# Sums and norms as stages of their own, a down product in two fp32r parts, and the next head's rows placed beside the linear attention

## The reference

```
x = x + xattn(layernorm(x), ctx, ctx)      # softmax attention, 16 heads of 16, 4096 keys
x = x + linear_attn(layernorm(x))          # causal; features exp(clip(norm(q) @ omega ...)), cumulative sums
x = x + ffn(layernorm(x))
# ffn: gate = x @ wg.T; up = x @ wu.T; h = silu(gate) * up; h @ wd.T
#      wg, wu: 768 x 256 and wd: 256 x 768, integers in -127..127, scaled by 1/127
```

## Time and profile before

| what | value |
|---|---|
| median of 3 timed runs | 877.69 us (876.39 to 878.99) |
| the profiled execution | 875.48 us |
| its span, first to last instruction | 873.8 us (873.76) |
| around the span | 1.7 us |
| PE busy | 829.1 us, 95% |
| PE weight loads busy | 569.8 us, 65% |
| ACT busy | 541.5 us, 62% |
| DVE busy | 417.2 us, 48% |
| POOL busy | 47.1 us, 5% |
| mean granted clock of TensorE | 0.990 |

### The profile page before, as it was taken

How to read it: one execution, slowest core, us unless ns; L and a number is a source line. 1 busy time by engine, 2 the same in 40 slices (tenths; PEclk the granted TensorE clock), 3 DMA queues, 4 the chain that set the end, 5 groups by cost and what they waited for, 6 DMA issues and landing times.

```text
span 873.8 us, 20543 instructions
## 1 busy us (share of the span) xinstructions
PE 829.1 (95%) x8817; PEld 569.8 (65%) x8817; DVE 417.2 (48%) x746; ACT 541.5 (62%) x598; POOL 47.1 (5%) x76
## 2 busy tenths in 40 slices
PE   6899999999999998999999998999999999989876
PEld 5666666666666666676666665667666666657656
DVE  7433236444644445534654446354474444402654
ACT  2478887776577665667567764575657666672141
POOL 1034000000000000000000000000000000000010
PEclk9899999999999999999999999999999999999999
DMA  7486654646344333346343441443614333202000
GB/s 248 172 258 237 241 183 166 209 158 193 122 146 146 142 125 133 122 133 191 136 146 145 146 142 53 158 158 129 195 65 170 122 122 119 100 2 50 0 2 15
DMA packets 58768, 120.08 MB, mean 137 GB/s; under 512 B 21552, under 2 KB 29744, under 8 KB 55152
## 3 DMA queue, kind: packets, MB, share of 16 engines
q1 hardware_dynamic: 56880, 114.31, 38.3%
q0 software_dynamic: 1792, 4.40, 1.7%
HBM read 78.84 MB, written 37.75 MB: 133 GB/s over the span
## 4 chain that ended last, share of the span: by engine, by line
PE 82%; DVE 8%; issue 4%; DMA 2%; ACT 2%; DVEq 1%; POOL 1%; SPq 0%; POOLq 0%; ACTq 0%
PE ps_o L816 26%; PE ps_s L828 18%; PE ps_pa L662 10%; PE ps_pa L617 10%; PE ps_pa L763 2%; PE ps_pa L692 2%; PE ps_pa L788 2%; PE ps_pa L775 2%; PE ps_pa L754 1%; ACT probs L1258 1%; PE ps_pa L740 1%; DMA oscr<-y 1%; PE ps_pa L684 1%; PE ps_pa L795 1%; PE ps_pa L767 1%
## 5 line engine op out<-in xcount | busy, mean ns | idle before, releaser
L1258 ACT ACTIVATE probs<-ps_s 128x1024 f32<-128x1024 f32 x512 | 496.8, 1023 | 234.2 <-PE ps_s L828 227.7
L816 PE MATMUL ps_o<-probs,values 128*17 128x256 f32 x4096 | 256.1, 385 | 0.0
L828 PEld LDWEIGHTS ps_s<-qstack,kstack 64*128 64x128 f32 x2048 | 140.0, 186 | 99.6 <-ACT probs L1258 48.8
L828 PE MATMUL ps_s<-qstack,kstack 64*128 64x256 f32 x2048 | 194.0, 307 | 5.3 <-ACT probs L1258 5.3
L816 PEld LDWEIGHTS ps_o<-probs,values 128*17 128x17 f32 x4096 | 104.1, 98 | 98.7 <-issue 9.8
L1343 DVE TENSOR_SCALAR kparts<-ps_pa,b_heads 128x512 fp32r<-128x512 f32 x64 | 48.0, 750 | 107.4 <-PE ps_pa L617 107.1
L662 PE MATMUL ps_pa<-wv_hi,ctx_hi 128*128 128x256 f32 x256 | 79.6, 311 | 2.9 <-DVE wv_lo L1331 2.2
L1360 DVE TENSOR_TENSOR values<-ps_pa,bv_pair 128x512 f32<-128x512 f32 x64 | 44.2, 690 | 77.5 <-PE ps_pa L662 77.1
L662 PE MATMUL ps_pa<-wv_lo,ctx_hi 128*128 128x256 f32 x256 | 72.5, 283 | 0.0
L662 PE MATMUL ps_pa<-wv_hi,ctx_lo 128*128 128x256 f32 x256 | 72.4, 283 | 0.0
L617 PE MATMUL ps_pa<-ctx_hi,wk_hi 128*128 128x512 f32 x128 | 56.4, 441 | 0.0
(11 more groups left out here) (274 smaller groups left out, 786.7 us busy)
## 6 DMA issues: line engine op xcount, KB each, us to landing
kstack<-kscr SPq DMA_DIRECT2D x96, 512.0 KB, 5.3
kscr<-kparts SPq DMA_DIRECT2D x64, 512.0 KB, 2.7
ctx_raw<-ctxT SPq DMA_DIRECT2D x32, 512.0 KB, 6.5
qstack<-qscr SPq DMA_DIRECT2D x12, 256.0 KB, 3.5
qscr<-qparts SPq DMA_DIRECT2D x4, 512.0 KB, 3.1
xh<-x SPq DMA_DIRECT2D x4, 256.0 KB, 5.4
kstack<-kstack SPq DMA_DIRECT2D x2, 512.0 KB, 6.0
qstack<-ksample SPq DMA_DIRECT2D x4, 256.0 KB, 3.6
```

The source lines that it names most:

```text
L816: last = mm(ps_o[32 * j:32 * j + DH + 1, g * S:(g + 1) * S], values[par][:, i, head_of_step(g, j), :], prob[:, j * S:(j + 1) * S], start=b ...
L828: last = mm(ps_s[s % 2][:, j * S:(j + 1) * S], kstack[par][rows, u, i * P:(i + 1) * P], queries[rows, u, :], start=True, stop=True)
L1258: nc.scalar.activation(probs[n % AHEAD][:, :], ps_s[n % 2][:, :], ACT.Exp, scale=float(DH) ** -0.5).then_inc(fast["exp_done"], 1)
```

## The change

Four things are done.

1. The sum and the layernorm become two stages. `wh` and `wout` end with the addition, so that `operand` counts there and the bank is free; `ln1` (step 13) and `ln2` (step 92) are DVE stages of their own right behind them. `ln1T` and `ln2T` wait for them.
2. `down` becomes fp32r: `wd_sb` is held as fp32r (its integers fit), the activations `hid` are cut into a high and a low fp32r part by a cast and a subtraction at the end of each `gate{k}`, and each of the 12 products becomes two. The parts of k = 0 to 3 lie in the query stack that is not in use, those of k = 4 and 5 in `x_parts`, which is why `gate4` and `gate5` wait for `gu5` on PE. The last tail does the same.
3. The stages move. The head's `ln0`, `ln0T` and `q` go from steps 86, 94 and 100 to 58, 68 and 72, among the units of the linear attention; the gates go to steps 99 to 111 (before: 99 to 121) and `down` from 124 to 115; `max0` to `maxT` shift by one or two steps. On SP the queries' stacking moves from chunk 6 to chunk 7 and waits for `down`.
4. The integers of wd are loaded into two tiles that are idle then, without waiting for a key stack; the square root of the features' weights moves in POOL's list to its place at step 80; the last tail has 4 fewer `warm` products.

```diff
-HEAD = ["ln0", "ln0T", "q", "kbd0", "max0", "max1", "kbd1", "max2", "max3", "maxT"]
+HEAD = ["ln0", "ln0T", "q", "kbd0", "kbd1", "max0", "max1", "max2", "max3", "maxT"]
...
-AT = {"o": 1, "oT0": 3, "oT1": 4, "yT": 12, "wh": 13, "ln1T": 19, "qk0": 20, "ss0": 20, "qk1": 22, "ss1": 22, "v": 24,
-      "norm0": 26, "norm1": 27, "qkT0": 28, "qkT1": 30,
+AT = {"o": 1, "oT0": 3, "oT1": 4, "yT": 12, "wh": 13, "ln1": 13, "ln1T": 19, "qk0": 20, "ss0": 20, "qk1": 22, "ss1": 22,
+      "v": 24, "norm0": 26, "norm1": 27, "qkT0": 28, "qkT1": 30,
       "feat0": 38, "feat1": 42, "A0": 46, "A1": 48, "pv0": 52, "feat2": 54, "A2": 58, "A3": 62, "feat3": 64, "pv1": 66,
-      "A4": 70, "A5": 74, "pv2": 76, "A6": 78, "A7": 80, "pv3": 84, "o2T0": 86, "o2T1": 88, "y2T": 90, "wout": 92,
-      "ln2T": 96, "gu0": 99, "gate0": 101, "gu1": 102, "gate1": 103, "gu2": 104, "gate2": 105, "gu3": 106, "gate3": 107,
-      "gu4": 110, "gate4": 111, "gu5": 120, "gate5": 121, "down": 124}
+      "A4": 70, "A5": 74, "pv2": 76, "A6": 78, "A7": 80, "pv3": 84, "o2T0": 86, "o2T1": 88, "y2T": 90, "wout": 92, "ln2": 92,
+      "ln2T": 96, "gu0": 99, "gate0": 100, "gu1": 100, "gu2": 102, "gate1": 102, "gu3": 104, "gate2": 105, "gu4": 106,
+      "gate3": 107, "gu5": 108, "gate4": 110, "gate5": 111, "down": 115}
...
-HEAD_AT = {"ln0": 86, "ln0T": 94, "q": 100, "kbd0": 106, "max0": 108, "kbd1": 110, "max1": 112, "max2": 115,
-           "max3": 116, "maxT": 118}
+HEAD_AT = {"ln0": 58, "ln0T": 68, "q": 72, "kbd0": 106, "kbd1": 110, "max0": 110, "max1": 112, "max2": 116,
+           "max3": 118, "maxT": 120}
...
+                    if b + 1 < B and p == HEAD_AT["maxT"] // STEPS:
+                        if b:
+                            sp.wait_ge(fast["product"], fast.at("product", tail_of(b - 1), "down"))
                         stack_queries(fast, b + 1, qstacks[(b + 1) % 2])
-                    if b + 1 < B and p == HEAD_AT["maxT"] // STEPS:
                         shift_queries(fast, head_of(b + 1), qstacks[(b + 1) % 2])
...
+                pe.wait_ge(c["operand"], c.at("operand", clock, f"gate{k}"))
                 for t in range(ST):
-
-                    last = mm(bank[:, t * D:(t + 1) * D], hid[:, k, t * P:(t + 1) * P], wd_sb[:, k, :],
-                              start=k + t == 0, stop=k == HB - 1, skip_group_check=True)
+                    for part in range(2):
+
+                        last = mm(bank[:, t * D:(t + 1) * D], hid_part(parts_of(c, clock), k, part)[:, t * P:(t + 1) * P],
+                                  wd_sb[:, k, :], start=k + t + part == 0, stop=k + part == HB, skip_group_check=True)
...
-            warm(ps_p, 26)
+            warm(ps_p, 22)
...
                 elif name in ("wh", "wout"):
-                    v.tensor_tensor(xs[:, :, :], xs[:, :, :], bank[:, :].rearrange("p (t d) -> p t d", t=ST), ALU.add)
-                    dve.drain()
+                    last = v.tensor_tensor(xs[:, :, :], xs[:, :, :], bank[:, :].rearrange("p (t d) -> p t d", t=ST), ALU.add)
+                elif name in ("ln1", "ln2"):
                     last = layernorm(c, name, clock)
...
-                    last = v.scalar_tensor_tensor(hid[:, n, :], gate_e[:, n % 2, :], 1.0, hid[:, n, :],
-                                                  ALU.add, ALU.mult)
+                    if n >= HALF // 2:
+                        dve.wait_ge(c["product"], c.at("product", clock, f"gu{HB - 1}"))
+                    of = parts_of(c, clock)
+                    v.scalar_tensor_tensor(hid[:, n, :], gate_e[:, n % 2, :], 1.0, hid[:, n, :], ALU.add, ALU.mult)
+                    dve.drain()
+                    last = cut(hid_part(of, n, 0), hid_part(of, n, 1), hid[:, n, :])
...
```

More of the change, by code:

```diff
@@ L134, in __init__ @@
             "operand": (head, TAIL),
-            "powered": (["ln0"], ["wh", "wout"]),
+            "powered": (["ln0"], ["ln1", "ln2"]),
             "acted": ([], FEATS + GATES), "kfeat": ([], FEATS),
@@ L168, in __init__ @@
         super().__init__(sem, prefix, HEAD)
-        self.order = [(0, n) for n in HEAD_FIRST]
+        self.order = [(0, n) for n in HEAD]
         for b in range(B):
@@ L291, in perceiver, with hid_part @@
         hid = flat_amat.rearrange("p (k s) -> p k s", s=S)
+        wd_int = [qk[:, :, :].rearrange("p t c -> p (t c)").bitcast(INT32).rearrange("p (k n) -> p k n", n=D),
+                  y[:, :, :].bitcast(INT32)]
         x_parts = [sb("x_hi", [P, CI, S], FP32R)[:, :, :], sb("x_lo", [P, CI, S], FP32R)[:, :, :]]
+        def hid_part(of, k, part):
+            n = 2 * k + part
+            return qstacks[of][:, n, :] if n < HALF else x_parts[(n - HALF) // CI][:, n % CI, :]
         gate_e, up = kfeat[:, 0, :, :], kfeat[:, 1, :, :]
@@ L369, in keys_bank, with parts_of @@
             return ps_a if (q, j) in ((0, 1), (1, 0), (1, 1), (2, 0)) else ps_p
+        def parts_of(c, clock):
+            return 0 if c is general else clock[1] % 2
         def head_of(b):
@@ L996, in last_down @@
                 for t in range(ST):
-                    last = mm((ps_p, ps_a)[t][:, 0:D], hid[:, k, t * P:(t + 1) * P], wd_sb[:, k, :],
-                              start=k == 0, stop=k == HB - 1)
+                    for part in range(2):
+                        last = mm((ps_p, ps_a)[t][:, 0:D], hid_part((B - 1) % 2, k, part)[:, t * P:(t + 1) * P], wd_sb[:, k, :],
+                                  start=k + part == 0, stop=k + part == HB)
                     if k == HB - 1:
@@ L1177, in _ @@
                 pool.dma_start(wu_int[k], wuT[k * P:(k + 1) * P, :]).then_inc(i_in, 16)
-            pool.wait_ge(fast["k_stacked"][1], 3 * STACKED)
-            pool.dma_start(wd_sb[:, :, :].bitcast(INT32), wr(wdT)).then_inc(i_in, 16)
+            for k, part in zip((0, HB - CI), wd_int):
+                n = part.shape[1]
+                pool.dma_start(part, wr(wdT)[:, k:k + n, :]).then_inc(i_in, 16)
             def weighted(c, f, clock):
@@ L1190, in stage @@
                     weighted(c, FEATS.index(name), clock)
-                elif name in ("ln0", "wh", "wout"):
+                elif name in ("ln0", "ln1", "ln2"):
                     power(c, name, clock)
-            pool.wait_ge(setup_pow, 1)
-            pool.tensor_tensor(node_amp[:, :], node_amp[:, :], root_power[:, :], ALU.pow).then_inc(setup_pow, 1)
             for b in range(B):
                 for step in range(BS):
+                    if b == 0 and step == SETUP_STEP:
+                        pool.wait_ge(setup_pow, 1)
+                        pool.tensor_tensor(node_amp[:, :], node_amp[:, :], root_power[:, :], ALU.pow).then_inc(setup_pow, 1)
                     for name, clock in stages_at(b, step):
@@ L1624, in setup_tail @@
                     v.tensor_copy(wu_r[:, k, :], wu_int[k])
-                v.tensor_copy(wd_sb[:, :, :], wd_sb[:, :, :].bitcast(INT32))
+                for k, part in zip((0, HB - CI), wd_int):
+                    v.tensor_copy(wd_sb[:, k:k + part.shape[1], :], part)
                 dve.drain()
@@ L1789, in _ @@
                 dve.drain()
-                v.scalar_tensor_tensor(hid[:, k, :], gate_e[:, k % 2, :], 1.0, hid[:, k, :], ALU.add, ALU.mult
-                                       ).then_inc(last_vector, 1)
+                v.scalar_tensor_tensor(hid[:, k, :], gate_e[:, k % 2, :], 1.0, hid[:, k, :], ALU.add, ALU.mult)
+                dve.drain()
+                if k >= HALF // 2:
+                    dve.wait_ge(*product_of(f"gu{HB - 1}"))
+                cut(hid_part((B - 1) % 2, k, 0), hid_part((B - 1) % 2, k, 1), hid[:, k, :]).then_inc(last_vector, 1)
             for t in range(ST):
```

13 lines of the change are left out of this document (5 added, 8 removed).

## The result

The changed kernel takes 892.91 us (median of 5 runs, 887.55 to 894.67), the kernel before 878.99 us beside it: ratio 1.015, 95% interval 1.0115 to 1.0185. It is slower by 1.5%. The forecast was 887.3 us with a range up to 892.5: sign and mechanism as forecast, the size 5.6 us short, just past the upper end of the range. As a ratio the forecast was 887.3 / 877.69 = 1.011 with an upper end of 1.017, and 1.015 lies inside, since the kernel before ran 1.3 us slower beside this one. The profiled execution took 887.55 us (span 885.8), 12.1 us more than the one of before.

A forecast was written before the change was run, and what follows sets the result against it. PE's nearly gapless list bounds the kernel; other engines cost only when PE waits. Middle tails +4.3 and +1.0, batch 3 -0.5, last tail +1.9 make +6.7; low clock makes +9.6: 885.1 profiled, 887.3 us timed, range 879 to 892.5.

The forecast's parts named there:

- Work removed from `down`: PE's `down` product as fp32r takes 3.0 us instead of 5.09, saving 2.1 us in each of three batches.
- Waits removed at `ln0T` and `gu1`: Middle tails: PE's waits of 2.33 or 2.68 us at `ln0T` and 0.66 at `gu1` go.
- Wait 1 before `gu0`: Middle tails: PE waits 2.1 us for `ln2T`'s cut, queued on DVE behind the split of the context.
- Wait 2 before `gu4`: Middle tails: PE waits 3.3 us for `gate2`, lengthened by its cut and queued behind a key unit on DVE.
- Waits 3 to 6: Middle tails: PE waits before `gu2`, `gu5`, a `max` stage and `down` (2.0 us) as DVE queues; together 3.5 us.
- Linear attention: Moved head stages on DVE delay PE by 0.6 us before `A3` and 0.65 before `A5`; sum 1.25.
- The last tail: After the last batch: DVE's cuts slow the gates by 2.6 us, fewer `warm` products return 0.6; sum +1.9 us.
- Batch 3: Longer waits before `gu4`, `gu2` and `down`, less work in `down`, partly hidden by ACT's pace: -0.5 us, between -1.1 and +1.5.
- The clock: Middle tails: new PE idles bring one stretch of low clock, 2.9 us; this forecast case had chance 0.32.
- the sum at the full clock: Whole kernel: both middle tails, batch 3 and the last tail together, without low clock, +6.7 us.
- The fourth rival: Low clock in both middle tails or more: 890.2 us with two stretches, 893 with three; chance 0.24.
- The first rival: The cut is covered, no new PE waits, idle before `gu4` under 0.5 us: -14.2 us, 863.5 us; chance 0.10.

The follow-up runs named there:

- run 1: Kernel before with only the layernorms as own stages, the head's `ln0`, `ln0T`, `q` moved earlier, and the matching loads and square root: 874.98 us, ratio 0.9961.
- run 11: Changed kernel with `down` in fp32 and no cut in any tail, all tables and stages still changed: 885.19 us, ratio 1.0077.
- run 3: Changed kernel with two DVE splits of the context one and two steps later in batches whose tail runs beside attention: 880.73 us, ratio 1.003.
- run 2: Changed kernel with `gate2` at step 104 instead of 105, ahead of that step's key unit: 884.78 us, ratio 1.0083.
- run 6: Changed kernel with `down` from the activations' high part alone, without cut, in tails beside attention; last tail keeps both parts: 875.33 us, ratio 0.9972.
- run 7: Changed kernel with PE running 12 unneeded products during its wait before `gu4`: 888.25 us, ratio 1.0127.
- run 9: Changed kernel with run 2's and run 3's edits, last `down` fp32 without cut, `gu4` two steps later and neighbouring stages shifted: 866.71 us, ratio 0.9868.

## Why the prediction fell short

**From before to after, by runs 1 and 11.** The medians give a staircase: before 878.3; moved rows alone 875.0; with the packed table 885.2 (this one has `down` in fp32); with the split `down` and its cut 892.9. So the rows gain 3.3 us, the packed table costs 10 and the split `down` 8, although it takes 6 us of work from PE. The last step is the least sure: in the profiled executions it is 0.9 us, and what the medians add to that stands and falls with the clock. Run 11 also has what else part 3 moves and the fewer `warm` products, which no run takes apart.

**The steps that held.** Work removed from `down`: 3.0 us forecast, 3.04 measured where the clock is full. Waits removed at `ln0T` and `gu1`: gone. Wait 1 before `gu0`: 2.1 forecast, 1.59 measured; `gu0` starts 10.5 us behind `wout` where 10.6 was forecast, but PE's own work between is 8.9, not 8.5. Its cause, the split of the context, is shown by run 3. Wait 2 before `gu4`: 3.3 and 3.22, and its two causes are shown by runs 2 and 6. Waits 3 to 6: 3.5 forecast, 3.2 in the first middle tail, with `down` at 2.0 and 1.97. Linear attention: 0.6 and 0.65 forecast, 0.64 and 0.57 measured. A cast of 256 columns takes 0.29 us (estimated 0.27).

**The last tail** was over-priced. From the first gate (869.58) to the end of the sixth cut (879.97) it is 10.4 us, 8.4 before: +2.0, where I had +2.6. Timeline of DVE after, the first gate, the end of the sixth cut, and the output:

```profile
869.58 0.42 DVE L1808 TENSOR_TENSOR amat<-kfeat,ps_s 128x256 f32<-128x256 f32 x1 [2.00 <-ACT kfeat L1327]
...
879.55 0.42 DVE L1346 TENSOR_TENSOR x_lo<-amat,x_lo 128x256 fp32r<-128x256 f32 x1
880.86 0.85 DVE L1817 SCALAR_TENSOR_TENSOR y<-ps_pa,xs 128x256 f32<-128x256 f32 x2 [0.89 <-PE ps_pa L1010]
```

The `warm` products give 0.9 back, not 0.6. The profiled executions agree on both prices: the last tail is 75.0 to 75.5 us long in the five runs that leave the cut out of it, and 77.1 to 77.4 in the four that have the cut and no low clock ahead of their last products (before, with 4 `warm` products more and no cut, 76.1). Batch 3 went the other way: the table below shows +0.3 where I had -0.5. The terms that the prediction writes out for it, 3.25 - 1.81 + 0.3 + 0.9 - 2.3, make +0.3; the step from there to -0.5 was a guess at what ACT's pace would hide, and the measured +0.3 shows nothing of it.

Lengths of the profiled executions by batch, us (the first three columns lie between starts of the same scores product in batches 1, 2 and 3 and the start of the last tail; then to the end):

| kernel | batch 1 | batch 2 | batch 3 | last tail | span |
|---|---|---|---|---|---|
| before | 203.5 | 206.5 | 67.2 | 76.1 | 873.8 |
| after | 209.8 | 205.9 | 67.5 | 78.6 | 885.8 |
| run 7, wait filled | 208.7 | 205.0 | 67.3 | 77.1 | 884.7 |
| run 11, `down` fp32 | 208.9 | 205.4 | 71.0 | 75.1 | 884.9 |
| run 9, `gu4` later | 201.7 | 199.3 | 67.0 | 75.0 | 869.6 |

Batch 2 of before holds the 2.95 us of low clock that the earlier trace rows show, and 2.05 us of the last head's `ln0T` and `q`, which the change moves ahead of that column's start; that is why it looks level.

**The step that failed is "The clock".** I took one stretch of low clock at 2.9 us, in place of the one of before. From the first middle tail on, the profiled execution has five ahead of the one at its very end, which before has too. Each is 3.4 us long but the last, of 6.8: two in the first middle tail, one in the second, one in batch 3 (before has one there too) and one in the last tail at 835 us. The new ones cost 3 x 1.5 + 1.6 = 6.1 us (an estimate: 1.5 from `down` above, 1.6 from the same run of products in the last tail before and after). Without them the difference of the profiled executions is 12.1 - 6.1 = 6.0 us, and the sum at the full clock had 6.7. So the sum was right to 0.7 us, and the term for the clock was less than half of what came. The timed runs have yet more of it: they lie 5 us above the profiled execution, at clocks of 0.974 to 0.977 against 0.981. By the slope, 0.010 of clock is 6.4 us of the 14.6 between the medians, and 8 us are waits. The forecast, put in the same way, had nothing for the clock and 9.6 for the waits (6.7, and the 2.95 of before).

The fourth rival was the one that came: "a low clock in both middle tails or more", with 893 us for three stretches. That this number is also the median measured is in part luck. Each stretch was priced at 2.9 us, from the one of before, which lasts 6.8 us (541.9 to 548.7); the three new ones in the middle tails last 3.4 us and cost 1.5 each. With the last tail's they come to 6.1 us where the rival had 8.7; the medians meet because the timed runs lie 5.4 us above the profiled execution, where the forecast had 2.2. My evidence for one was two idles of before, one with a stretch and one without; a second stretch of before, in batch 3 at 780.8 us behind an idle of only 0.89, I had left out. I should have priced it as a rate: six new idles of 1.6 us and more over two tails, at one in two, are three stretches. By the Trainium skill ("TensorE: Matmul & The Clock Gate", "A second HAM failure mode: psum-queue depth-cycling") PE's short idles between groups of matmuls can make the clock fall and rise over and over, and throughput is lost each time. The runs agree, with 26 stretches behind 46 idles of 1.5 to 3.2 us (last section). The prediction cited the section ahead of it in the same page of the Trainium skill ("HAM oscillation — how this bites in real kernels"), whose example has waits of 3 to 5 us; here shorter ones did it, and the measurement decides.

**The first rival's threshold** fits from the other side. It said that the change pays if the idle before `gu4` is under 0.5 us. Run 9 makes it so in both middle tails, with the split `down`, and takes 866.7 us; the rival had 863.5. It is no test of the threshold alone, since run 9 also removes the waits of `gu0` and `down` and the cut of the last tail.

**What stays open.** Runs 3 and 6 gained 2 and 3 us more than their waits and clocks give. The split between clock and waits goes by a correlation; only run 7 changes the clock with the waits left alone, and its size is uncertain. The first 325 us vary by some 3 us between profiled executions (the low clock of the start lasts 6.8 to 17 us in them), which I did not study.

## What to carry to other kernels

Where an engine sets the pace through one list, ask of each stage that is packed closer what stands ahead of its releaser on the helping engine's own list: a helper that is half idle can still be late by 3 us, and moving its instructions that nobody waits for (here two splits) behind those that somebody waits for can be free, as it was in run 3. Price a cluster of idles on PE twice, once for itself and once for the clock behind it, as a rate times the number of idles; filling one idle with useless products shows that the second price is there. A cheaper product that needs a new step on another engine should be put where its input has time to arrive, not packed with its producers.

## What the runs showed of the hardware

The granted clock in the middle tails of the 13 profiled executions: there are 26 stretches at half clock (24 of 3.4 us, two of 6.8), and each begins within 2 us of the start of a record that had waited 1.5 us or more. No stretch begins anywhere else in these tails, and run 9, whose longest idle there is 1.27 us, has none. Of the 46 such idles, by length:

| idle before the record | idles | followed by a stretch |
|---|---|---|
| 3.2 us | 8 | 7 |
| 2.3 to 2.8 us | 8 | 6 |
| 2.0 us | 10 | 8 |
| 1.5 to 1.75 us | 20 | 5 |

All ten idles of 2.0 us stand before `down` and all eight of 3.2 before `gu4`, so these are rates of places as much as of lengths. They hold for the middle tails only: in batch 3 and in the last tail stretches also began behind shorter idles, in the kernel before at 780.8 us behind one of 0.89, after at 835.2 behind one of 1.33.

That an idle of 2 us costs 1.5 us more in four cases of five I had not expected; from the two idles of before I had taken 2.3 us as harmless and 2.7 as the edge. The same idle at the same place (3.22 us before `gu4`) called a stretch in the first middle tail of the changed kernel and not in the second, so a single profile does not tell the rate.
